# Attention: the query norm's scaling moved behind the last pass over the spikes, and one division for each group of heads

## The chip, the cores and the metric

The kernel runs on one core of a Trainium2 chip. The metric is the device time of one execution in microseconds (us). Five engines work side by side, each with its own instruction stream, and meet in semaphores: TensorE (PE; its weight loads are PEld), VectorE (DVE), ScalarE (ACT), GpSimd (POOL) and SyncE (SP), which issues the DMAs.

## The reference

One decoder layer on x (8 sequences of 512 tokens, 256 features) in three residual steps. The first is a bidirectional Mamba block with its feed-forward part. The second and third are what matters here:

```
# second: cross attention, 16 heads of 16 features, over ctx (8, 512, 256)
q = layernorm(x) @ wq.T + bq;  k = ctx @ wk.T + bk;  v = ctx @ wv.T + bv
scores = where(mask == 0, -1e9, einsum('bhqd,bhkd->bhqk', q, k) / 4)
x = x + einsum('bhqk,bhkd->bhqd', softmax(scores), v) @ wo.T + bo
# third: a spiking network, 5 steps
y = square(relu(layernorm(x) @ W_fc.T)) @ W_proj.T
mem_new = 0.9 * mem + y - (mem > 1);  spk = mem_new > 1     # five times from mem = 0
x = x + sum(spk) / 5
```

## The kernel before

A first pass does the Mamba block for all sequences and takes some 1600 us. A second, `attention_pass`, does the feed-forward part of the first step, the attention and the spiking network, one sequence (a "batch", `b` from 0 to 7) after the other. The order on every engine is written out by hand: each engine has its own function `batch(b, it, more)`, and `more` is true for the first seven, which also prepare batch b+1. Batch 0 is written out on VectorE, batches 1 to 6 run in a loop, batch 7 is written out.

In a batch TensorE first computes the scores of all 16 heads once (`prescore`), of which VectorE takes row maxima (line 1912), while the feed-forward part of the next batch is woven in. Then come eight units of four heads by half of the keys. For each, TensorE computes the scores transposed (`score`), ScalarE takes the exponential (line 1696, shown as 1633), VectorE masks one half of the keys (`keep_exp`, line 1903), and TensorE multiplies by V (`weigh`), which also gives the sum of each row from a column of ones. After each two units a group of four heads is complete: TensorE transposes it to tokens (`to_tokens`, line 1517) and VectorE divides by the sums (`normalise`, lines 1797 to 1809) into o_sb, which the trace calls x_out.

Between the masks VectorE works on other things: the spikes of the previous batch (`start`, `step`, `finish`, over tiles y_sb, mem, cnt, tmp), and the norm of the next batch's query (`norm_apply(ATT, b + 1, x1n, xn_q)`, four operations at line 1750). `finish` (line 1842) writes tmp and raises out_ready.

Behind the units TensorE projects the next batch's K in two halves (`project_k`), transposes the attention's output and then the next query (both `to_features`, line 1388), multiplies by wo, and projects V and Q. ScalarE evacuates the last group (`av`), the two halves of K into qk, the transposes into xT, in this order. The four PSUM banks for all this go round in a fixed order; the second transpose of the output uses the bank of K's first half.

The tiles mem, cnt and tmp share their memory with qk. So ScalarE's `project_k` waits until SP has stored tmp:

```
act.wait_ge(out_ready.sem, out_ready.count(beta - 1))   # ACT, line 1660
act.wait_ge(s_out.sem, s_out.count(beta - 1))           # line 1661
sp.wait_ge(out_ready.sem, out_ready.count(beta))        # SP, store(), line 1317
```

SP's order in a batch is: loads for b+2, the rows of maxima, this store, then the writes and reads that stack K and Q.

Of the kernel before, what the change touches and what calls it, by code (L numbers as in the profile page):

```python
# [14 lines left out]
H, DH = 16, 16  # L15
P = 128
KD, KI, KF, TT = D // P, DI // P, FF // P, T // P
# [64 lines left out]
def attention_keys():  # L82

    def many(kind, n):
        return [(kind, i) for i in range(n)]

    ff = many("w1", KF)
    heads = []
    for g in range(H // 4):
        heads += [("av", g)] + ([("ot", g - 1)] if g else [])  # L90
    before = many("w2", 2) + many("k", KD) + [("lo", 0)] + many("qn", KD) + many("q", KD) + [("lo", 1)] + many("v", 2)
    loop = many("hT", KD) + ff + [("w2", 0), ("mt", 0), ("w2", 1), ("mt", 1)] + heads + [("k", 0), ("ot", H // 4 - 1), ("k", 1)]
    loop += many("on", KD) + many("qn", KD) + many("wo", 2) + [("v", 0)] + many("q", KD)
    loop += many("fn", KD) + [("v", 1)] + many("fc", KF) + many("pr", 2)
    skip = ("hT", "w1", "w2", "k", "v", "qn", "q")
    return before, loop, [key for key in loop if key[0] not in skip]
# [1075 lines left out]
def attention_pass(nc, ctx, a, mid, out, sb, where, stage, psum, consts, handover, early, late):  # L1172

    f32, bf16, i32 = mybir.dt.float32, mybir.dt.bfloat16, mybir.dt.int32
    ALU, ACT, AX = mybir.AluOpType, mybir.ActivationFunctionType, mybir.AxisListType
# [15 lines left out]
    x1n = sb("x1n", [P, TT, D])  # L1191
    x1 = sb("x1", [P, TT, D])
    x_res = sb("x_res", [P, TT, D])
    xn_q = sb("xn_q", [P, TT, D])
# [15 lines left out]
    rsum = sb("rsum", [P, TT, 4])  # L1210
# [25 lines left out]
    G = Ring(general + [y_bank], kinds, B - 1, *attention_keys())  # L1236
# [15 lines left out]
    FF1, ATT, FF2 = range(3)  # L1252
# [20 lines left out]
    with nc.Block() as block:  # L1273
# [451 lines left out]
        def _(dve):  # L1725
# [6 lines left out]
            def norm_stats(n, src):  # L1732

                dve.drain()
                for j in range(TT):
                    dve.bn_stats(stats[:, j, :], src[:, j, :])  # L1736
                norm_mean(n)

            def norm_mean(n):

                dve.drain()
                for j in range(TT):
                    last = dve.bn_aggr(mv[:, j, :], stats[:, j, :])  # L1743
                last.then_inc(ln_stats[n].sem, 1)

            def norm_apply(n, beta, src, dst):

                dve.wait_ge(ln_rstd[n].sem, ln_rstd[n].count(beta))
                for j in range(TT):
                    last = dve.tensor_scalar(dst[:, j, :], src[:, j, :], mv[:, j, 0:1], rstd[:, j:j + 1],  # L1750
                                             ALU.subtract, ALU.mult)
                last.then_inc(ln_out[n].sem, 1)

            def two(ap, jj):
                return ap[:, 2 * jj:2 * jj + 2, :]

            def bank_tiles(bk):
                return bk[:, :].rearrange("p (j f) -> p j f", j=2)

            def first_norm(beta):  # L1760
                dve.wait_ge(s_x.sem, s_x.count(beta))
                settle(dve)
                norm_stats(FF1, x0)
                norm_apply(FF1, beta, x0, xn)

            def add_down(beta, it):

                dve.wait_ge(x1n_set.sem, x1n_set.count(beta))
                for jj in range(TT // 2):
                    dve.wait_ge(*G.full(("w2", jj), it))  # L1770
                    bk = G.bank(("w2", jj), it)
                    dve.tensor_tensor(two(x1n, jj), two(x1n, jj), bank_tiles(bk), ALU.add).then_inc(G.done_sem(("w2", jj)), 1)  # L1772

            def cut_lo(beta, n):
                dve.wait_ge(qk_hi.sem, qk_hi.count(4 * beta + 2 * n))
                dve.tensor_tensor(qk[:, n], qk[:, n], qk_part[:, n, 0], ALU.subtract).then_inc(qk_lo.sem, 1)

            def cut_last(beta, n):
                dve.wait_ge(qk_hi.sem, qk_hi.count(4 * beta + 2 * n + 1))
                dve.tensor_tensor(qk_part[:, n, 2], qk[:, n], qk_part[:, n, 1], ALU.subtract).then_inc(s_part.sem, 1)  # L1780
# [16 lines left out]
            def normalise(g, it):  # L1797

                dve.drain()
                dve.wait_ge(*G.full(("ot", g), it))  # L1800
                bk = G.bank(("ot", g), it)
                o = bk[:, :].rearrange("p (j h e) -> p j h e", j=TT, h=4)
                dve.reciprocal(rsum[:, :, :], o[:, :, :, DH:DH + 1].squeeze(3))
                dve.drain()
                dst = o_sb[:, :, g * 4 * DH:(g + 1) * 4 * DH].rearrange("p j (h e) -> p j h e", h=4)
                for j in range(TT):
                    last = dve.tensor_tensor(dst[:, j], o[:, j, :, 0:DH],
                                             rsum[:, j, :].unsqueeze(2).broadcast_to((P, 4, DH)), ALU.mult)
                last.then_inc(G.done_sem(("ot", g)), 1)

            def spikes(beta, cols_of=(A3,)):

# [48 lines left out]
            last = dve.tensor_scalar(keep_bf[:, :, :], maskT_i[:, :, :], 0.0, None, ALU.not_equal)  # L1861
# [29 lines left out]
            for j in range(TT):  # L1891
                last = dve.tensor_scalar(mask_bias[:, j, :], keep[:, j, :], row_keep[:, j:j + 1], None, ALU.mult)
# [5 lines left out]
            def keep_exp(b, unit):  # L1898

                kt = 2 * (unit % 2) + 1  # L1900
                dve.wait_ge(s_exp.sem, s_exp.count(b * 2 * H + unit * 4 + ON_DVE[-1]))
                exps = pr[:, ON_DVE[0]:ON_DVE[-1] + 1, kt, :]
                dve.scalar_tensor_tensor(exps, mask_biasT[:, kt, :].unsqueeze(1).broadcast_to((P, len(ON_DVE), T)), -MASKED, exps,  # L1903
                                         ALU.add, ALU.min).then_inc(s_kept_dve.sem, 1)

            def batch(b, it, more):
                for hd in range(H):
                    for j in range(TT):
                        dve.wait_ge(s_max.sem, s_max.count((b * H + hd) * TT + j - 2))
                        dve.wait_ge(s_pre.sem, s_pre.count((b * H + hd) * TT + j))  # L1910
                        settle(dve)
                        dve.tensor_tensor_reduce(  # L1912
                            masked[:, j % 2, :], bank[j], mask_bias[:, j, :], 1.0, FLOOR, ALU.add, ALU.max, m_col[:, j, hd:hd + 1]).then_inc(s_max.sem, 1)
                start, step, finish = spikes(b)
                if more:
                    add_down(b + 1, it)
                    norm_stats(ATT, x1n)
                start()
                step(1, (0,))
                keep_exp(b, 0)  # L1920
                step(1, (1, 2))
                keep_exp(b, 1)
                if more:
                    norm_apply(ATT, b + 1, x1n, xn_q)
                step(2, (0,))
                keep_exp(b, 2)
                step(2, (1, 2))
                if isinstance(it, int):
                    dve.wait_ge(early.mid.sem, early.mid.count(B))
                keep_exp(b, 3)  # L1930
                normalise(0, it)
                step(3, (0,))
                keep_exp(b, 4)
                step(3, (1, 2))
                keep_exp(b, 5)
                normalise(1, it)
                step(4, (0,))
                keep_exp(b, 6)
                step(4, (1, 2))
                keep_exp(b, 7)  # L1940
                finish()
                normalise(2, it)
                normalise(3, it)
                if more:
                    cut_lo(b + 1, 0)

                dve.wait_ge(x1_set.sem, x1_set.count(b))
                for jj in range(TT // 2):
                    dve.wait_ge(*G.full(("wo", jj), it))
                    bk = G.bank(("wo", jj), it)  # L1950
                    dve.tensor_tensor(two(x_res, jj), two(x1, jj), bank_tiles(bk), ALU.add).then_inc(G.done_sem(("wo", jj)), 1)
                    dve.drain()
                    for j in (2 * jj, 2 * jj + 1):
                        dve.bn_stats(stats[:, j, :], x_res[:, j, :])
                norm_mean(FF2)
                if more:
                    cut_last(b + 1, 0)
                    take_v(0, it)
                norm_apply(FF2, b, x_res, xn)
                if more:  # L1960
                    take_q(it)
                    cut_lo(b + 1, 1)
                    take_v(1, it)
                    cut_last(b + 1, 1)
                    dve.wait_ge(*G.done(("fn", KD - 1), it))
                    first_norm(b + 2)
# [224 lines left out]
```

## Time and profile before

| | us |
|---|---|
| median of 3 runs | 2731.34 |
| lowest and highest | 2731.16, 2732.35 |
| the profiled execution | 2730.98 |
| its span, first to last instruction | 2729.2 |
| TensorE busy | 2585.1 (95%) |
| VectorE busy | 2283.9 (84%) |
| ScalarE busy | 1743.3 (64%) |
| GpSimd busy | 1602.4 (59%) |

Times in the rows are counted from the span's start. A busy time includes work that nothing waits for, and a wait is put down to the one of several releasers that the profile shows last. A line can be that of a helper: 1380 is every matmul, 1633 every ScalarE operation of this pass, 1283 every DMA.

### The profile page before, as it was taken

The page shows a single profiled execution, that of the slowest core. Times are in us where ns is not written, and L with a number is a line of the kernel's source. Part 1 is how long each engine was busy: PE and PEld are TensorE (multiplying, and loading weights), DVE is VectorE, ACT ScalarE, POOL GpSimd, SP SyncE. Part 2 cuts the span into 40 slices and gives each one's busy share as a digit, 9 for nine tenths or more (in the row PEclk, how much of TensorE's full clock was granted, in tenths as well). Part 3 has the DMA queues.
Part 4 walks back from the last instruction along what each step waited for, and adds up shares of the span by engine and source line. Part 5 has one row for each costly group of instructions (what it writes and reads, how often), then busy time and mean ns, then how long its engine had stood idle before and what let it go on. Part 6 is the DMA issues. An engine that isn't in the chain of part 4 may idle for free. (4 is left out here: it accounts for less than half of the span.)

```text
span 2729.2 us, 54786 instructions
## 1 busy us (share of the span) xinstructions
PE 2585.1 (95%) x18901; PEld 1767.7 (65%) x18934; DVE 2283.9 (84%) x3333; ACT 1743.3 (64%) x2871; POOL 1602.4 (59%) x886
## 2 busy tenths in 40 slices
PE   6999999999999999999998888999999999999995
PEld 3887787787777778777787764455454545454523
DVE  5999999999999899999999949686869595959684
ACT  4878877877977888788788633635354545444342
POOL 3999999999999999999999932111111111111010
PEclk9999999999999999999999999999999999999978
DMA  3122212212221221222122042404040404040300
GB/s 124 43 74 79 82 48 79 92 36 72 89 72 52 81 82 44 71 82 80 50 77 98 17 152 87 114 11 123 2 123 2 123 2 123 2 123 2 108 2 16
DMA packets 102089, 187.07 MB, mean 69 GB/s; under 512 B 14720, under 2 KB 75264, under 8 KB 100256
## 3 DMA queue, kind: packets, MB, share of 16 engines
q1 hardware_dynamic: 101840, 183.92, 21.4%
q8 instruction: 135, 2.21, 0.3%
q14 instruction: 114, 0.93, 0.1%
HBM read 148.38 MB, written 35.52 MB: 67 GB/s over the span
## 5 line engine op out<-in xcount | busy, mean ns | idle before, releaser
L983 DVE TENSOR_TENSOR_SCAN h<-dA,pair 128x512 f32<-128x512 f32 x1024 | 1172.6, 1201 | 101.9 <-PE pair L476 90.6
L1122 POOL TENSOR_TENSOR hC<-h,C_rep 128x1024 f32<-128x1024 f32 x512 | 1200.8, 2370 | 72.2 <-DVE h L983 64.5
L720 ACT ACTIVATE dA<-delta,cols 128x511 f32<-128x511 f32 x1024 | 664.2, 710 | 33.8 <-DVE h L983 27.7
L476 PE MATMUL pair<-diagB,duT 64*128 64x128 f32 x8192 | 549.3, 281 | 24.9 <-DVE h L983 15.6
L476 PEld LDWEIGHTS pair<-diagB,duT 64*128 64x128 f32 x8192 | 486.4, 188 | 126.8 <-issue 96.9
L577 PE MATMUL y_bank<-ident,hC 128*128 128x128 f32 x3980 | 521.6, 277 | 12.4 <-POOL hC L1122 10.5
L577 PEld LDWEIGHTS y_bank<-ident,hC 128*128 128x128 f32 x3980 | 440.3, 141 | 105.1 <-issue 50.5
L1912 DVE CUSTOM_DVE_ANT_0 masked<-pair,mask_bias 128x512 f32<-128x512 f32 x512 | 321.8, 687 | 19.9 <-PE pair L1380 13.6
L1999 POOL TENSOR_SCALAR rstd<-mv 128x4 f32<-128x4 f32 x24 | 23.8, 992 | 453.5 <-DVE mv L1743 451.6
L1633 ACT ACTIVATE pr<-pair 128x1024 f32<-128x1024 f32 x256 | 248.4, 1022 | 50.3 <-PE pair L1380 50.2
L2028 POOL CAST m_part<-m_rest 8x512 bf16<-8x512 f32 x16 | 9.7, 604 | 415.2 <-ACT m_rest L1633 415.2
L476 PE MATMUL general<-xnT,w_in 128*128 128x512 f32 x496 | 243.0, 605 | 4.5 <-ACT xnT L720 3.6
L1380 PE MATMUL general<-w_down,g 128*128 128x256 f32 x1024 | 232.5, 380 | 1.3 <-DVEq L1728 1.3
L1380 PEld LDWEIGHTS general<-w_down,g 128*128 128x128 f32 x1024 | 193.7, 190 | 33.8 <-issue 5.9
L1380 PE MATMUL pair<-q_st,k_st 99*128 99x512 bf16 x512 | 178.5, 385 | 8.2 <-ACT pr L1633 4.7
L1380 PE MATMUL general<-xT,w_up 128*128 128x512 f32 x360 | 167.2, 601 | 1.2 <-ACT xT L1633 0.7
L1903 DVE SCALAR_TENSOR_TENSOR pr<-mask_biasT,pr 128x2048 f32<-128x2048 bf16 x64 | 153.0, 2390 | 8.5 <-ACT pr L1633 8.5
L1380 PE MATMUL pair<-k_st,q_st 96*128 96x512 bf16 x512 | 152.3, 405 | 6.0 <-DMA q_st<-qk_parts 4.2
L993 DVE SCALAR_TENSOR_TENSOR u<-general,cols,u 128x511 f32<-128x511 f32 (+2 forms) x192 | 141.7, 738 | 14.2 <-ACT u L720 10.2
L1380 PEld LDWEIGHTS pair<-q_st,k_st 99*128 99x128 bf16 x512 | 50.3, 98 | 141.4 <-ACT pr L1633 96.4
L1972 DVE COPY y_sb<-general 128x512 f32<-128x512 f32 x16 | 11.1, 691 | 139.6 <-PE general L1380 139.6
L1380 PEld LDWEIGHTS pair<-k_st,q_st 96*128 96x128 bf16 x512 | 50.1, 98 | 113.0 <-DVE m_col L1912 80.0
(185 smaller groups left out, 3240.5 us busy)
## 6 DMA issues: line engine op xcount, KB each, us to landing
C_rep<-c_rows SPq DMA_DIRECT2D x128, 512.0 KB, 4.0
qk_parts<-qk_part SPq DMA_DIRECT2D x96, 256.0 KB, 4.1
w_in<-w_in SPq DMA_DIRECT2D x16, 1024.0 KB, 4.8
k_st<-qk_parts SPq DMA_DIRECT2D x8, 1536.0 KB, 9.1
q_st<-qk_parts SPq DMA_DIRECT2D x8, 1536.0 KB, 9.4
x_in<-x SPq DMA_DIRECT2D x18, 512.0 KB, 4.1
w_out<-w_out SPq DMA_DIRECT2D x17, 512.0 KB, 4.3
mid<-x_out SPq DMA_DIRECT2D x9, 512.0 KB, 4.8
```

The lines of the kernel that those rows point to most:

```text
L476: return pe.matmul(o, lhsT, rhs, start=start, stop=stop)
L577: last = pe.matmul(y_bank[:, c * P:(c + 1) * P], hC[:, g % RING, i, c * P:(c + 1) * P], ident[:, :], start=j == 0 and i == 0 and c == 0, s ...
L720: return act.activation(o, i, fn, **kw)
L983: last = dve.tensor_tensor_scan(h[:, g % 4, i, :], dA[:, g % 4, i, :], dBu[:, i, :], 0.0, ALU.mult, ALU.add)
L993: dve.scalar_tensor_tensor(u[n][:, k, lag:T], raw[:, 0:T - lag], col("fb"[n] + "conv_w", CW * k + CW - 1 - lag), u[n][:, k, lag:T], ALU.mu ...
L1122: last = pool.tensor_tensor(hC[:, g % RING], h[:, g % 4], C_rep[:, 2 * j:2 * j + 2, :], ALU.mult)
L1380: return pe.matmul(o, lhsT, rhs, start=start, stop=stop)
L1633: return act.activation(o, i, fn, **kw)
L1903: dve.scalar_tensor_tensor(exps, mask_biasT[:, kt, :].unsqueeze(1).broadcast_to((P, len(ON_DVE), T)), -MASKED, exps, ALU.add, ALU.min).the ...
L1912: dve.tensor_tensor_reduce(masked[:, j % 2, :], bank[j], mask_bias[:, j, :], 1.0, FLOOR, ALU.add, ALU.max, m_col[:, j, hd:hd + 1]).then_in ...
L1972: dve.tensor_copy(two(y_sb, jj), bank_tiles(bk)).then_inc(G.done_sem(key), 1)
L1999: pool.tensor_scalar(rstd[:, :], mv[:, :, 1], EPS, None, ALU.add)
```

## The change

Two edits, both on VectorE. In `normalise` four multiplications, one for each block of 128 tokens, become one over 4 blocks x 4 heads x 16 features. In `batch` the query norm's four operations go from between the masks of units 1 and 2 to behind `finish`, and the division of group 2 goes from behind `finish` to ahead of it. The order at the end was mask 7, finish, normalise(2), normalise(3); it is now mask 7, normalise(2), finish, query norm, normalise(3).

```
@@ normalise
-                for j in range(TT):
-                    last = dve.tensor_tensor(dst[:, j], o[:, j, :, 0:DH],
-                                             rsum[:, j, :].unsqueeze(2).broadcast_to((P, 4, DH)), ALU.mult)
-                last.then_inc(G.done_sem(("ot", g)), 1)
+                dve.tensor_tensor(dst, o[:, :, :, 0:DH], rsum[:, :, :].unsqueeze(3).broadcast_to((P, TT, 4, DH)),
+                                  ALU.mult).then_inc(G.done_sem(("ot", g)), 1)
@@ batch
                 keep_exp(b, 1)
-                if more:
-                    norm_apply(ATT, b + 1, x1n, xn_q)
                 step(2, (0,))
@@ batch
                 keep_exp(b, 7)
+                normalise(2, it)
                 finish()
-                normalise(2, it)
+                if more:
+                    norm_apply(ATT, b + 1, x1n, xn_q)
                 normalise(3, it)
```

## Rows read from the trace of the kernel before

**Rows 1.** Page, busy time, share of the span and instructions of each engine

```profile
PE 2585.1 (95%) x18901; PEld 1767.7 (65%) x18934; DVE 2283.9 (84%) x3333; ACT 1743.3 (64%) x2871; POOL 1602.4 (59%) x886
```

**Rows 2.** Waits: us in total, times, longest us

```profile
ACT qk L1633 <- DMA out<-tmp: 20.1, 7, 2.9
```

**Rows 3.** Chain of waits, end of batch 2: start us, us, what

```profile
1997.21 1.03 ACT pr L1633
...
1998.27 2.30 DVE pr L1903
...
2000.61 1.07 PE y_bank L1380 x8
2001.68 1.91 PE general L1380 x4
...
2005.75 1.31 PE general L1388 x12
2007.06 0.44 PE y_bank L1388 x4
...
2007.51 3.73 PE general L1380 x16
```

**Rows 4.** Timeline of VectorE, batch 2: start us, us, operation, idle before

```profile
1969.47 2.28 DVE L1903 SCALAR_TENSOR_TENSOR pr<-mask_biasT,pr 128x2048 f32<-128x2048 bf16 x1
1971.67 1.38 DVE L1750 TENSOR_SCALAR xn_q<-x1n,mv,rstd 128x256 f32<-128x256 f32 x4
1973.14 1.22 DVE L1828 SCALAR_TENSOR_TENSOR tmp<-mem,y_sb 128x1024 f32<-128x1024 f32 x1
...
1979.10 2.28 DVE L1903 SCALAR_TENSOR_TENSOR pr<-mask_biasT,pr 128x2048 f32<-128x2048 bf16 x1
1981.56 0.26 DVE L1803 RECIPROCAL rsum<-general 128x16 f32<-128x16 f32 x1 [0.17 <-issue]
1981.89 0.62 DVE L1807 TENSOR_TENSOR x_out<-general,rsum 128x64 f32<-128x64 f32 x4
1982.60 1.23 DVE L1828 SCALAR_TENSOR_TENSOR tmp<-mem,y_sb 128x1024 f32<-128x1024 f32 x1
...
1998.27 2.28 DVE L1903 SCALAR_TENSOR_TENSOR pr<-mask_biasT,pr 128x2048 f32<-128x2048 bf16 x1
2000.65 1.23 DVE L1842 SCALAR_TENSOR_TENSOR tmp<-cnt,x_res 128x1024 f32<-128x1024 f32 x1
...
2004.07 0.26 DVE L1803 RECIPROCAL rsum<-general 128x16 f32<-128x16 f32 x1 [1.08 <-PE general L1517]
...
2009.58 0.68 DVE L1951 TENSOR_TENSOR x_res<-x,general 128x512 f32<-128x512 f32 x1
```

**Rows 5.** Timeline of SyncE's DMA issues, end of batch 2

```profile
2002.17 0.41 SPq L1283 DMA_DIRECT2D out<-tmp  x1
```

**Rows 6.** Timeline of ScalarE, end of batch 2

```profile
2005.22 0.69 ACT L1633 ACTIVATE qk<-general,cols 128x512 f32<-128x512 f32 x1 [2.87 <-DMA out<-tmp]
2005.80 0.68 ACT L1633 ACTIVATE qk<-y_bank,cols 128x512 f32<-128x512 f32 x1
2006.37 1.08 ACT L1633 ACTIVATE xT<-general 128x512 f32<-128x512 f32 x2
```

**Rows 7.** Line 1807 over the span: duration ns min/median/max, first and last start

```profile
L1807 DVE TENSOR_TENSOR x_out<-general,rsum x128: 211/215/226, 1714.8 to 2668.4; 128x64 f32<-128x64 f32 x128
```

**Rows 8.** Timeline of VectorE, batch 0, behind the mask of unit 3

```profile
1712.07 2.28 DVE L1903 SCALAR_TENSOR_TENSOR pr<-mask_biasT,pr 128x2048 f32<-128x2048 bf16 x1
1714.44 0.26 DVE L1803 RECIPROCAL rsum<-general 128x16 f32<-128x16 f32 x1
```

**Rows 9.** Chain of waits, end of batch 7

```profile
2667.98 0.63 DVE x_out L1807 x4
```

**Rows 10.** Windows: stretch, length, busy us of PE, PEld, DVE, ACT, POOL, PEclk, DMA

```profile
2000.00:2003.00 3.00, 2.39 (x11) 0.83 (x12) 2.66 (x7) 0.60 (x1) 0.00 (x0) 1.00 0.00 0
2665.00:2680.00 15.00, 7.18 (x39) 5.03 (x40) 7.79 (x26) 1.68 (x3) 1.26 (x2) 0.93 0.11 36
```

## The prediction

> **What bounds the kernel now.** I read the page first, then the waits, then the chain of waits through one batch, then each engine's timeline around the two places that the change touches. In the page TensorE is busy 95% of the span and VectorE 84% [rows 1]: a VectorE saving counts only where TensorE is waiting for VectorE, and an average cannot say where that is. In the waits the reader is to see one row: seven times, 2.9 us at the longest, ScalarE stood still before its write to qk until the store out<-tmp had landed [rows 2]. qk shares its memory with mem, cnt and tmp, so each of the seven batches that prepare a next one has this wait.
>
> The chain from 1997 to 2008 us is batch 2, and the batches before and after repeat it to a few hundredths. The exponentials of the last unit end at 1998.24, the mask over them (keep_exp 7) starts at 1998.27, weigh at 2000.61, then TensorE runs without a gap through K, the transposes of group 3, K again, and the transposes of line 1388, to 2007.50; the output projection starts at 2007.51 [rows 3]. Two paths end there. ScalarE's starts with the store: `finish` ends at 2000.65 + 1.23 = 2001.88 [rows 4], SP issues the store at 2002.17 [rows 5], ScalarE, idle for 2.87 us, begins K's first evacuation at 2005.22, and then works back to back (5.22, 5.80, 6.37, each 0.57 to 0.58 apart) until both xT evacuations end at 2007.45 [rows 6]. The projection needs these. So against TensorE's 2007.50 the store path has no slack worth counting: what is added to it moves the projection, and with it the residual, the second norm and the spiking network, which follow one from another.
>
> **The norm that moves (4 operations, 1.38 us).** It stands between the mask of unit 1 and step 2: the norm starts at 1971.67 and step 2 at 1973.14, where without it step 2 would start 0.09 after the mask's end at 1971.75, so it takes 1.30 us of VectorE's time there [rows 4]. Could this make the stretch shorter? Only if VectorE is still late at its end. It is not: the mask of unit 7 starts 0.03 us after the exponentials that it waits for [rows 3], VectorE has caught up by then, and an earlier start of units 2 to 5 becomes waiting for exponentials. I cost this part at nothing; if VectorE were the pacer, its whole 1.30 us would be the gain (rival 1). In the new place, behind it on VectorE stands normalise(3), counted below; its reader is query_input on TensorE, in the second half of the transposes of line 1388; its own wait for rstd is met already at the present place, some 30 us earlier.
>
> **The order of finish and normalise(2).** Before: mask ends at 2000.55, finish starts at 2000.65 (0.10 later). After: normalise(2) comes first. Its drain and wait cost what they cost behind unit 3's mask, where the mask ends at 1979.10 + 2.28 = 1981.38 and the reciprocal starts at 1981.56: 0.18. Then the reciprocal and the gap behind it, 1981.89 - 1981.56 = 0.33 [rows 4]. Then the one multiplication.
>
> **The one multiplication.** The trace has no 128x256 form of it, so it is bounded. Below by one 128x64 operation, 0.215 us [rows 7]; above by the four together, 0.62 us [rows 4]. Between them: 64 elements take 0.215 and the 128x512 tensor_tensor from PSUM of line 1951 takes 0.68 [rows 4, 7], so an element costs (0.68 - 0.215)/448 = 1.04 ns, and 256 take 0.215 + 192 x 1.04 ns = 0.42 us. I take 0.42; four small ones overlapped in 0.62, so 0.20 us is saved at each of the 32 calls. Groups 0 and 1 lie under TensorE's continuous work and give nothing.
>
> The trace has the four at 0.62 us, less than 4 x 0.215 = 0.86, so they hide part of each other's fixed time [rows 4, 7]. The Trainium skill (VectorE: DVE Perf Modes, "The TRN2 errata — SBUF-src ops pay a fixed extra latency per instruction") says that the fixed latency is exposed between instructions, so that many small tiles pay it each time, and gives (N+151)/0.96 ns for an fp32 tensor_tensor. An estimate by that page is 424 ns for the merged one and 3 x 157 ns = 0.47 us saved per call; the sum below would end 0.27 us lower, as only the last batch's tail takes it from this term, and the row for the four speaks against that larger saving.
>
> **The sum for finish.** New start of finish behind the mask's end: 0.18 + 0.33 + 0.42 + 0.09 (the gap behind normalise, from 1981.89 + 0.62 to 1982.60) [rows 4] = 1.02, against 0.10 now: 0.92 later. In batch 0, whose waits are on constants, the first gap is 1714.44 - (1712.07 + 2.28) = 0.09 instead of 0.18 [rows 8], so 0.83. The store is issued and lands that much later, and so ScalarE's K evacuation starts at 2006.14 instead of 2005.22.
>
> Does something swallow it? On TensorE the second "on" transpose takes the bank of K's first half, which ScalarE frees at 2006.14 + 0.69 = 2006.83; four transposes later (0.6 us) it is full at about 2007.45, before ScalarE comes to it at about 2007.86. So ScalarE stays back to back, ends at 2008.37, and the projection starts at about 2008.43, with TensorE idle for the difference. Nothing else ends on an absolute time there: the exponentials, masks and DMAs of K and Q all follow from this start.
>
> ScalarE's 2.87 us before K is a wait for a store and nothing else [rows 2, 6]. The Trainium skill (DMA: Bandwidth & Descriptors, "Rules for kernel authors") says to issue a DMA early and wait for its semaphore late, so that its fixed cost overlaps; this change does the reverse, putting work ahead of the issue while the waiter stays where it is. By that rule too the time comes out above the present one, and the trace agrees in that the landing ends that wait in seven of seven batches.
>
> **normalise(3).** Finish ends at 2000.55 + 1.02 + 1.23 = 2002.80. The norm starts 0.08 before that (as behind the mask, 1971.67 against 1971.75) and ends at 2004.10; with 0.17 the reciprocal is at 2004.27 against 2004.07 now, and the multiplication ends at 2004.27 + 0.33 + 0.42 = 2005.02, where the four end now (2004.07 + 0.33 + 0.62) [rows 4]. No change; and the transposes of line 1388 now have most of a microsecond to spare before ScalarE wants them.
>
> **The last batch** has no norm and no K to evacuate, so the late store costs nothing there. Its chain runs through normalise(3), whose multiplications take 0.63 us there before the transposes [rows 9]. In either order the same operations stand ahead of it, less 0.20 us for group 2, so VectorE comes to it no later than now, and the shorter multiplication counts: -0.2.
>
> **Sum.** 0.83 + 6 x 0.92 - 0.2 = 6.15 us, on a profiled execution of 2730.98 (span 2729.2, the rest around it unchanged). The profiled run lies 0.36 below the median of 2731.34; carried to the median, 2737.5 us. The unknown multiplication gives the narrow range: at 0.215 it is 1.4 less in seven batches and 0.2 less in the last, 2735.9; at 0.62 it is 1.4 more, and the last saving is gone, 2739.1.
>
> **Rivals.** Rival 1, faster: VectorE is the pacer of the spikes stretch. Taking 1.30 us out before unit 2 then brings the last mask 1.30 forward, more than the 0.92 that the store loses; net 0.38 per batch, 7 x 0.38 + 0.2 = 2.9, so 2728.5. It decides from the point where the last mask starts more than 0.92 earlier relative to the exponentials. For it: it is busy 84% of the span, and more in this stretch than in most. Against it: the 0.03 us at the last mask, where ScalarE is the releaser [rows 3].
>
> Rival 2, no change: the store was hidden anyway, the wait put down to it having really ended with something else, such as TensorE's K in y_bank. Then only the -0.2 is left, 2731.1. For it: TensorE ends K's second half at 2005.75, close to its evacuation at 2005.80 [rows 3, 6]. Against it: the first half was complete at 2001.68 + 1.91 = 2003.59, and its evacuation waited 1.6 us more, until the store landed.
>
> Rival 3, slower still: the merged operation, with its three strides and its broadcast, costs what the four cost or more, or the longer gap takes something from TensorE's clock. The price of the first is 2739.1. For the clock: it stayed at 1.00, that is 2.4 GHz, in the three microseconds with the 1.1 us gap before weigh, and showed 0.93 only where TensorE was busy for 7.18 of 15 us [rows 10]; an added gap of 0.9 us is nearer to the first.
>
> **Chances.** Forecast 0.76, rival 1 0.06, rival 2 0.10, rival 3 0.08. The time is the forecast's, 2737.5. The range for 8 in 10 is 2734.0 to 2739.5: it holds the forecast with its bounds and most of rival 3, goes a little towards rival 2 for a partial cover of the store, and leaves out the rest. 0.2%, about what a measurement of this kernel can tell from no change, is 5.5 us, and the lower part of the forecast's range lies within that. So faster 0.06, same 0.10 + 0.14 of the forecast's 0.76 = 0.24, slower 0.70.
>
> **What would show it.** Right: finish ends some 2.25 us behind the last mask's end instead of 1.33; out<-tmp is issued 0.9 us later relative to that mask, and ScalarE's idle time before qk grows from 2.9 to about 3.8 us; the projection of w_att and xT starts about 10.2 us behind the last mask's start instead of 9.24, with a new TensorE idle time before it that ScalarE's xT ends; line 1807 has 32 rows of 128x256 at about 0.42; a batch takes 0.9 us more. The masks of units 2 to 5 start earlier, the last one does not. Wrong: if the last mask stands earlier against its exponentials, rival 1; if the store moves and the projection does not, rival 2; if line 1807 shows 0.6 or more, or the clock falls between 2003 and 2009 us, rival 3. A span that is less than 4 us longer would mean that a cover exists which I have not seen.

## The result, and the profile after

The kernel after takes 2741.2 us at the median of 11 runs (2735.37 to 2745.24), the one before 2731.52 (2728.81 to 2733.72, 11 runs): a ratio of 1.0033 with a 95% interval of 1.0025 to 1.0041, about 9 us more. The profiled execution took 2741.24 us, its span is 2739.5 us, 10.3 more than before. The forecast was 2737.5 in 2734.0 to 2739.5: the right way, and too small.

The chain of waits of the kernel after through the end of batch 2 (start, us, what) answers to [rows 3]:

```profile
1997.42 1.03 ACT pr L1633
...
1998.48 2.29 DVE pr L1901
...
2000.93 0.26 DVE rsum L1803
...
2001.26 0.42 DVE x_out L1806
...
2001.78 1.24 DVE tmp L1840
...
2003.31 2.94 DMA out<-tmp
...
2006.35 0.70 ACT qk L1633
...
2007.09 1.09 PE general L1388 x8
2008.19 0.44 PE y_bank L1388 x4
...
2008.65 3.50 PE general L1380 x15
```

Before, this chain went through TensorE's own queue. It now leaves the mask through the division of group 2 and through `finish` into the store, and comes back to TensorE through ScalarE's K evacuation. From the mask's start to the projection it takes 2008.65 - 1998.48 = 10.17 us, against 9.24. The timelines of VectorE, ScalarE and TensorE in the same place answer to [rows 4, 6]:

```profile
1998.48 2.29 DVE L1901 SCALAR_TENSOR_TENSOR pr<-mask_biasT,pr 128x2048 f32<-128x2048 bf16 x1
2000.93 0.26 DVE L1803 RECIPROCAL rsum<-general 128x16 f32<-128x16 f32 x1 [0.16 <-issue]
2001.26 0.42 DVE L1806 TENSOR_TENSOR x_out<-general,rsum 128x256 f32<-128x256 f32 x1
2001.78 1.23 DVE L1840 SCALAR_TENSOR_TENSOR tmp<-cnt,x_res 128x1024 f32<-128x1024 f32 x1
2002.92 1.38 DVE L1750 TENSOR_SCALAR xn_q<-x1n,mv,rstd 128x256 f32<-128x256 f32 x4
2004.47 0.26 DVE L1803 RECIPROCAL rsum<-general 128x16 f32<-128x16 f32 x1 [0.16 <-PE general L1517]
```

```profile
2006.35 0.69 ACT L1633 ACTIVATE qk<-general,cols 128x512 f32<-128x512 f32 x1 [3.80 <-DMA out<-tmp]
2006.94 0.68 ACT L1633 ACTIVATE qk<-y_bank,cols 128x512 f32<-128x512 f32 x1
2007.51 1.09 ACT L1633 ACTIVATE xT<-general 128x512 f32<-128x512 f32 x2
```

```profile
2007.09 0.66 PE L1388 MATMUL general<-ident,x_out 128*128 128x128 f32 x4 [0.70 <-ACT qk L1633]
```

The merged multiplication takes 0.42 us, `finish` ends 2.24 us behind the last mask, and ScalarE waits 3.80 us instead of 2.87. TensorE stands still 0.70 us ahead of the second "on" transpose, until ScalarE frees its bank. That is its only added wait: ahead of the projection the weight loads wait 0.26 us for xT, and in the kernel before 0.25. Two paths meet at the projection again, TensorE's transposes (to 2008.63) and ScalarE's xT (to 2008.60).

But a batch is longer by more than these 0.93 us. The store's issue marks one point in every batch: 1868.66 and 2003.31 here, so 134.65 us apart; before, 1868.66 and 2002.17, 133.51 apart. The six periods differ by 1.12 us each. The other 0.19 is in the stage of the maxima. The timeline of VectorE after, batches 1 to 3, shows the same pause there in each:

```profile
1811.01 0.69 DVE L1910 CUSTOM_DVE_ANT_0 masked<-pair,mask_bias 128x512 f32<-128x512 f32 x1 [0.41 <-issue]
...
1945.65 0.69 DVE L1910 CUSTOM_DVE_ANT_0 masked<-pair,mask_bias 128x512 f32<-128x512 f32 x1 [0.42 <-issue]
...
2080.29 0.69 DVE L1910 CUSTOM_DVE_ANT_0 masked<-pair,mask_bias 128x512 f32<-128x512 f32 x1 [0.42 <-issue]
```

"Issue" says that the engine waited for nothing that the profile shows. The kernel before has no such pause in its loop. Two more of this kind stand in the kernel after. The first is in batch 0 alone, ahead of `finish`, and makes the store there later: it is issued 5.09 us behind the mask's start instead of 3.90, and the projection starts at 10.43 instead of 9.25, so batch 0 loses 1.18 us. The second is in every batch of the loop, ahead of the reciprocal behind the mask of unit 3, where the kernel before has 0.17:

```profile
1732.51 1.23 DVE L1840 SCALAR_TENSOR_TENSOR tmp<-cnt,x_res 128x1024 f32<-128x1024 f32 x1 [0.45 <-issue]
...
1981.08 0.26 DVE L1803 RECIPROCAL rsum<-general 128x16 f32<-128x16 f32 x1 [0.52 <-issue]
```

And the last batch is longer too: from its last mask's start to the end 2739.5 - 2668.2 = 71.3 us, before 2729.2 - 2662.8 = 66.4. Windows over its last mask, then the output projection, then the first W_fc matmuls (columns as in [rows 10]), first after, then before:

```profile
2668.20:2677.00 8.80, 5.41 (x31) 2.66 (x29) 4.87 (x7) 1.79 (x3) 0.00 (x0) 0.74 0.18 60
2677.00:2683.50 6.50, 6.44 (x16) 4.86 (x16) 1.46 (x4) 0.00 (x0) 0.00 (x0) 0.57 0.00 0
...
2691.20:2699.10 7.90, 7.90 (x13) 3.47 (x14) 0.00 (x0) 2.45 (x4) 0.00 (x0) 0.68 0.00 0
```

```profile
2662.80:2670.50 7.70, 4.08 (x32) 1.62 (x30) 5.29 (x13) 1.68 (x3) 0.00 (x0) 1.00 0.20 68
2670.50:2674.20 3.70, 3.70 (x16) 2.94 (x16) 1.44 (x3) 0.00 (x0) 0.00 (x0) 1.00 0.00 0
...
2682.00:2688.80 6.80, 6.79 (x13) 3.08 (x14) 0.00 (x0) 2.45 (x4) 0.00 (x0) 0.79 0.00 0
```

The same sixteen matmuls take 6.5 us at a clock of 0.57 (near 1.2 GHz) and 3.7 at 1.00 (2.4 GHz).

So the 10.3 us between the two profiles have three parts: -2.3 up to the last mask of batch 0, 7.7 from there to the last mask of batch 7, 4.9 from there to the end. The first part lies ahead of every instruction that the change touches: in the profiles of all thirteen kernels here this mask starts between 1728.2 and 1733.9 us, and always 58.1 us behind the same row of maxima, so the difference arises before that row, and the first division comes later. What makes it is open.

### The profile page after: what moved, and what is told of

It reads as the page before. It is cut to its first block and busy times, and to the rows that moved or that the text cites. A ratio compares the mean times of both kernels' runs of the same rounds, so it can differ in the third digit from the quotient of the medians.

```text
span 2739.5 us, 54723 instructions
## 1 busy us (share of the span) xinstructions
PE 2589.7 (95%) x18934; PEld 1769.4 (65%) x18934; DVE 2278.6 (83%) x3237; ACT 1743.3 (64%) x2871; POOL 1602.1 (58%) x886
```

## The experiments

Four theories. S: the loss is the store, issued behind more work while ScalarE waits for it ahead of K. R: it is the norm's or the division's own cost. I: the 0.19 us per batch is a pause of VectorE's instruction supply, which depends on where its code lies. C: what is left is TensorE's clock in the last batch. Ratios are against the kernel before on the same chip.

**The swap alone.**

```
                 keep_exp(b, 7)
+                normalise(2, it)
                 finish()
-                normalise(2, it)
                 normalise(3, it)
```

> The kernel before with one edit: normalise(2) stands ahead of finish; four multiplications, and the query norm, stay as they were. Theory S (the late store): finish comes 0.18 + 0.33 + 0.62 + 0.09 - 0.10 = 1.12 us later behind the last mask, so out<-tmp is issued 5.0 us behind that mask's start instead of 3.9, ScalarE waits 4.0 us for it instead of 2.9, the projection starts 10.4 us behind the mask instead of 9.24, and each of seven batches is 1.1 us longer: 7.8 us in all. Theory R (the moved norm or the merged division makes the loss): no change. Theory C (TensorE's clock in the last batch makes what lies above 6.5 us): 7.8 us as in S, and more only if the profile shows half the clock behind the last batch's masks.

Measured: 2742.21 us (5 runs), ratio 1.0038 [1.0024, 1.0051]. The store is issued 5.02 us behind the mask's start, ScalarE waits 4.00 us for it, the projection starts 10.36 behind, the periods are 134.63, 1.12 more: every length as S has it. There is no pause among the maxima in the loop, and in the last batch of its profile the clock is near half over the output projection (0.57), which may be what lies above 2731.1 + 7.8 = 2738.9. The swap alone makes a loss as large as the whole change; with four multiplications ahead of `finish` the store alone costs 1.12 us a batch, with the one it is 0.93.

**The norm alone.**

```
                 keep_exp(b, 1)
-                if more:
-                    norm_apply(ATT, b + 1, x1n, xn_q)
...
                 finish()
                 normalise(2, it)
+                if more:
+                    norm_apply(ATT, b + 1, x1n, xn_q)
                 normalise(3, it)
```

> The kernel before with one edit: the query norm goes behind normalise(2), ahead of normalise(3), and finish stays directly behind the last mask. Theory S: the store is issued as before (3.9 us behind the mask's start), so only normalise(3) can be late: the norm ends near 6.0 us behind the mask's start, normalise(3) near 7.15 instead of 6.75, the transposes wait some 0.3 us, and a batch is 0.3 us longer, 2 us in all. Theory R: the whole loss of the change, 1.1 us per batch, stands here. Rival 1 of the prediction (VectorE is the pacer): faster by up to 1.3 us per batch.

Measured: 2731.33 (11 runs), 1.0002 [0.9993, 1.0011], periods of 133.51. R is out for the norm, and so is the prediction's first rival: 1.30 us taken from the spikes' stretch brought nothing. My own 0.3 us was wrong: normalise(3) does end 7.12 us behind the mask's start instead of 6.75, as worked out, but the transposes start 7.31 behind, as before. There was more slack there than I had read from the weight loads.

**The division alone**, as in the first part of the diff.

> The kernel before with one edit: one multiplication of 128x256 in each normalise. Theory S: the store and the projection stay where they are; the last batch saves 0.2 us; no change in all. Theory I (VectorE has 12 operations fewer in a batch, its code lies elsewhere, and the stall of 0.42 us among the maxima in each batch of the loop comes from that): that stall, shown as masked <- issue, appears here too, and a batch is up to 0.2 us longer, 1.3 us in all. Against I: no such stall, period 133.5 us.

Measured: 2732.3 (11 runs), 1.0003 [0.9994, 1.0012]. In the total nothing is seen, but the periods are 133.71 instead of 133.51, with the pause of 0.42 us in every batch of the loop: the first sign for I. It comes with the merge, not with the moves, and so does the one ahead of `finish` in batch 0 (0.44 us; the projection starts 9.59 us behind the mask instead of 9.25). The second pause of the loop, ahead of the reciprocal, is not here; e4 below has it with the same period, so it costs nothing that shows. The division as work of the engine costs nothing either, and R is out for it too.

**The store waited for where it must be.** The kernel after with

```
 def project_k(beta, it):
-    act.wait_ge(s_out.sem, s_out.count(beta - 1))
...
 for k in range(KD):
     evacuate(("on", k), xT[1][:, k, :], it)
 if more:
+    act.wait_ge(s_out.sem, s_out.count(b))
     high(b + 1, 0)
```

> The kernel after, but ScalarE's wait for the store moves from ahead of its K evacuations to ahead of the first copy into qk_part, which is what shares memory with tmp; K's half of qk shares it with mem alone, and mem is read for the last time before out_ready. Theory S: ScalarE evacuates K's first half when finish is done (near 2.3 + 2.25 - 0.0 = 4.6 us behind the mask's start, instead of 7.9), the projection starts 9.25 us behind the mask as in the kernel before, and the loss of 0.93 us per batch is gone: 6.5 us less than the kernel after, so 0 to +3 against the one before. What is left is the 0.19 us per batch of the maxima's stall (1.3 us) and, by theory C, the clock in the last batch (up to 4 us in one run). Rival (the loss sits in the transposes' late input, not in the store): as slow as the kernel after.

The timeline of ScalarE in batch 2 of this kernel; its last mask starts 5.36 us before the first line:

```profile
2004.03 0.69 ACT L1633 ACTIVATE qk<-general,cols 128x512 f32<-128x512 f32 x1 [1.29 <-PE general L1380]
2006.18 0.69 ACT L1633 ACTIVATE qk<-y_bank,cols 128x512 f32<-128x512 f32 x1 [1.47 <-PE y_bank L1380]
2006.77 1.07 ACT L1633 ACTIVATE xT<-general 128x512 f32<-128x512 f32 x2
```

K is now evacuated when TensorE has made it. The store is still issued 4.82 us behind the mask's start, as late as in the kernel after, and the projection starts 9.23 behind, as in the kernel before; periods are 133.70. The 0.93 us are gone though every VectorE operation stands where the change put it, which settles S. The total is 2736.58 (11 runs), 1.0017 [1.0008, 1.0026], some 4.6 us above the kernel before, where 6 x 0.19 = 1.1 are the pause. The rest is not in the periods; the profile has 1.7 us of it behind the store that is issued in batch 7 (below, "the last store"; two half-size ones follow at the very end).

**The instruction stream as long as before.** The kernel after with

```
 dve.tensor_tensor(dst, o[:, :, :, 0:DH], ...)
+for _ in range(TT - 1):
+    settle(dve)          # a semaphore increment
```

> The kernel after, with three semaphore increments (sequencer instructions, no work of the engine) behind each merged multiplication, so that VectorE's instruction stream is as long as before at the same places. Theory I (the stall of 0.42 us among the maxima in each batch of the loop comes from where VectorE's code lies, the stream being shorter by three instructions at each normalise): the stall is gone, a batch takes 134.45 us instead of 134.64, and 1.3 us are gone in all. Rival (it comes from the moved norm, or from the timing of the batch): the stall stays, at the same place; e3 with the merged division alone speaks against that. A third outcome: the increments cost some 0.05 us each on the way to finish, and the store is later by up to 0.15 us, a batch longer by as much.

Measured: 2736.89 (9 runs), 1.0022 [1.0012, 1.0032]. All three pauses are gone, in batch 0 and in the six batches of the loop; the periods are 134.42, 0.21 less, and batch 0's projection starts 10.09 us behind the mask, 0.84 later than in the kernel before. In its profile TensorE's clock is 1.00 over the last output projection (16 matmuls in 3.72 us), and from the last store to the end it takes 62.57 us, as in the kernel before. The store is issued 4.83 us behind the mask's start, so the increments cost nothing that shows. The same in the kernel with the division alone:

> e3 (the merged division alone) with three semaphore increments behind each merged multiplication, as in e5. Theory I: no stall among the maxima in the loop, a batch takes 133.51 us as in the kernel before instead of 133.71, and with the store in its place nothing else is left: 2731.0 plus or minus 1. If the merged division itself cost something: 133.7 us.

Measured: 2730.98 (11 runs), 0.9994 [0.9985, 1.0003], periods of 133.52. So the part of I that was tested holds: twelve instructions more or fewer per batch turn the pause off and on. That it is a wait for code is argued only. Which instruction meets it, and whether it is the code's address or the distance between two loads of code, I did not separate. The Trainium skill (Runtime: NRT & Kernel Launch, "Instruction fetch mechanics") says that each engine's sequencer fetches its code in blocks with DMAs of its own, and that crossing a block is mostly hidden. Here, if that is what the pause is, 0.42 us of it showed in each batch, 0.19 to 0.21 of which reached the period.

**The last batch as before.** The kernel after, but with the old order and the four multiplications in batch 7:

```
+if more:
+    normalise(2, it); finish(); norm_apply(ATT, b + 1, x1n, xn_q)
+else:
+    finish(); normalise(2, it)
```

> The kernel after, but in the last batch alone the order (finish, then normalise(2)) and the four multiplications are as before. Theory P (the last batch is slower in the kernel after, 4 us in its profile, because the clock's falls land at another moment, which the earlier batches' length decides): as slow as the kernel after, 2741, low mean clock in as many runs, and half the clock in the profile behind the last masks. Rival L (the last batch's own order or its merged operation does it): the time falls by about 2 us at the median and the clock behind the last masks is 1.00 as in the kernel before.

Measured: 2742.09 (5 runs), 1.0042 [1.0028, 1.0056], with the clock over the output projection near half again. The last batch's own edits are not what makes it slow.

**TensorE kept busy in the last batch.**

```
 def prescore(b, hd):
+    if isinstance(b, int) and b == B - 1:
+        mm(bank[j], ...)                    # each prescore twice
...
+if not more:
+    pe.wait_ge(*G.free(("fn", 0), it))
+    for _ in range(16):
+        mm(G.bank(("fn", 0), it)[:, :], ident_bf[:, :], mask_biasT[:, 0, :])
 pe.wait_ge(ln_out[FF2].sem, ln_out[FF2].count(b))
```

> The kernel after, with TensorE kept busy in the last batch alone: each prescore matmul is issued twice, and 16 matmuls of 128x512 bf16 go into the bank of the norm's transposes before it is waited for; outputs are unchanged. Theory C (what lies above 7 x 1.12 us in the kernel after is TensorE at 1.2 instead of 2.4 GHz behind the last masks): the clock shows 1.00 from the prescores of the last batch to the end of its matmuls but for the last spikes, the spread of the runs shrinks to 5 us or less, and the median falls by 3 to 6 us, to 2735 to 2738. If the clock were no cause, the median stays at 2741 or rises by what the added matmuls take (up to 1 us).

Windows of this kernel over the output projection and the first W_fc matmuls:

```profile
2673.40:2677.10 3.70, 3.68 (x16) 3.11 (x18) 1.44 (x3) 0.00 (x0) 0.00 (x0) 1.00 0.01 4
...
2684.00:2689.40 5.40, 5.39 (x13) 2.52 (x14) 0.00 (x0) 2.45 (x4) 0.00 (x0) 1.00 0.00 0
```

Measured: 2734.59 (11 runs), 1.0017 [1.0008, 1.0026], 4.4 us below the kernel after by the ratios and 6.6 by the medians (two chips), with more matmuls than it has. From the last store to the end it takes 59.35 us, where the kernel after takes 66.75 and the one before 62.67. The maxima gain too: the last store comes 129.40 us behind the one before it, against 130.92. The spread did not shrink as expected (2731.55 to 2739.98), so the clock in the last batch is not all that makes it. The same added to the kernel before:

> The kernel before with TensorE kept busy in the last batch as in e7. Theory C: the last batch is worth the same to both kernels once the clock is at 2.4 GHz, so what is left between this and e7 (2734.6) is the seven batches' 7 x 1.12 = 7.8 us less 0.2 to 0.4 for the last batch's shorter division: 2727.0. From its parts: issue to issue as in the kernel before (133.5), the last store to the end 59.5 us instead of 62.7. If the clock's fall were tied to the kernel after alone, this would stay at 2731.

Measured: 2729.59 (11 runs), 0.9988 [0.9979, 0.9997], 2.6 above what I expected; the last store to the end is 60.41 us in the profile, not 59.5. So the clock costs the kernel before something as well. With it kept up, after and before are 1.0017 - 0.9988 = 0.0029 apart, 7.9 us, where the lengths in the traces give 6 x 1.12 + 1.18 - 0.2 = 7.7; without, 0.0033, 9.0 us. The clock's share of the difference is thus about 1 us by the ratios, and 3 by the medians (9.7 - 6.4); with intervals of some 2.5 us on each ratio, that it is more than nothing isn't shown.

**A version below both.** Two paths end at the projection, so both must be shortened. The kernel before, with ScalarE's wait as in e4, and half of K's first projection in the gap in which TensorE waits for the last mask:

```
 if unit + 1 < H // 2:
     score(b, unit + 1, half)
+elif more and half == 1:
+    project_k_part(b + 1, 0, 0, it)      # K's first half, k = 0
 weigh(b, unit, half, it)
...
 if more:
-    project_k(b + 1, 0, it)
+    project_k_part(b + 1, 0, 1, it)      # k = 1
```

> The kernel before (its order on VectorE untouched), with ScalarE's wait for the store ahead of its first copy into qk_part, as in e4, and on TensorE the first half of K's first projection (k = 0, 0.86 us) ahead of the last weigh, where TensorE stands still 1.13 us for the last mask. Theory S (two paths end at the projection, the store's and TensorE's own): both are shortened by this, the projection starts 8.4 to 8.5 us behind the last mask's start instead of 9.24, a batch takes 132.7 us, and the kernel 5.5 us less than before, 2725 to 2726, less what the clock in the last batch adds (up to 4 us in a run). If the store were no bound: the same. If ScalarE's evacuation of the last group now ends last: 9.0 to 9.2 us, and 1 us gained at most.

TensorE's timeline there; the last weigh no longer shows a wait:

```profile
1995.90 1.13 PE L1380 MATMUL general<-ctxT,w_att 128*128 128x512 f32 x2
1997.10 1.07 PE L1380 MATMUL y_bank<-pr,v_sb 128*32 128x512 f32 x8
1998.10 1.12 PE L1380 MATMUL general<-ctxT,w_att 128*128 128x512 f32 x2
```

Measured: 2728.13 (11 runs), 0.999 [0.9981, 0.9999]; the projection starts 8.37 us behind the mask's start and the periods are 132.64, 0.87 less. Of the 6.1 us in seven batches only 2.8 reach the median: from the last store to the end the profile shows 67.68 us instead of 62.67. With TensorE kept busy in the last batch as well:

> e8 (half of K's projection in TensorE's gap, the store waited for later) with TensorE kept busy in the last batch as in e7. Both parts are in different batches and add up: 6 periods of 132.64 instead of 133.52 us, and the last store to the end 59.5 us instead of 62.7: 2721 to 2722, some 9.5 us below the kernel before. If the clock eats the gain of e8 in another way: 2725 or more.

Measured: 2722.68 (6 runs), 0.9967 [0.9955, 0.9979], 9 us below the kernel before, which makes this version the fastest of all. From the last store to the end its profile has 62.09 us, not the 59.5 expected: the clock was not 1.00 throughout.

## Why the prediction was wrong in size and right in kind

1. That ScalarE's wait for the store sets the pace at the end of a batch, with no slack against TensorE's own path: right. Shown by e1 (the swap alone makes the loss) and e4 (moving the wait alone takes it away). Rival 2 is out.
2. The lateness of `finish`, 0.92: right, measured 0.93 in the loop. In batch 0, 0.83 was forecast; without the pauses it is 0.84 (e5), with them 1.18. ScalarE's K was due 7.87 us behind the mask's start and started 7.87 behind in batch 2; the multiplication was taken at 0.42 and took 0.42. The added wait of TensorE is not ahead of the projection, where the prediction put it, but ahead of the second "on" transposes, at K's bank; the time of the projection comes out the same (10.17 us behind the mask's start, 10.16 forecast).
3. The moved norm at nothing: right (e2). The last masks start 0.03 us behind their exponentials in both kernels; what VectorE gained became waiting, such as 0.76 us ahead of the mask of unit 6. Rival 1 is out.
4. normalise(3) at no change: right for its effect, and with more room than I claimed (e2).
5. The step that failed is the sum, in "the rest around it unchanged": it put everything outside the edited stretch at nothing, without a reason. Two things changed there. The merged division made VectorE's instruction stream shorter, and pauses appeared: 0.42 us among the maxima of each batch in the loop, of which 0.19 reached the period, and 0.45 ahead of `finish` in batch 0, of which 0.35 reached the projection; 6 x 0.19 + 0.35 = 1.5 us in all. I had counted the edit's instructions as engine time only, not as code. Shown by e3, e5 and e11. Without the pauses the kernel after is at 1.0022, which is 6.0 us, where the forecast had 6.15. That this comes so close is in part luck: the interval is 2.7 us to either side, and the profile of e5 has the clock at 1.00 over the last output projection, as the kernel before has.
6. The second thing is the clock. The last batch was put at -0.2; in the profile it took 4.9 us more from its last mask to the end, where the output projection ran at 0.57. The clock stood in rival 3, as something that an added gap in the middle might take. In the middle it stayed at 1.00. The prediction read that the kernel before showed less than 1.00 only where TensorE was busy for 7.18 of 15 us; that overlooks the last batch's maxima, where both kernels have 0.50 from 2600 to 2610 us with TensorE busy throughout. What the clock adds to the difference of the medians is not fixed: 1 to 3 us, and nothing is within the intervals. That the last batch's own edits are not the cause is shown (e6 has the fall without them, e5 has them without the fall); it is not the pauses either, as e1 has the fall and no pause. That the length of the earlier batches decides, by moving the moment, fits e3, e6 and e8, whose profiles have near half the clock too with no common edit in that batch, and is argued only, from one profile of each.
7. The range ended at 2739.5, 1.7 us below the median. It was built from the terms of the sum alone. The spread of single runs, 5 us before and 10 us after, was not in it, and up to the last mask of batch 0 alone single profiles differ by 5.7 us.

## What to carry to other kernels

A write that another engine waits for, through a buffer that two tiles share, belongs ahead of work that nobody waits for; and the wait belongs ahead of the first instruction that touches the shared bytes, not ahead of the stage. Before counting a VectorE saving, look at what ends the wait behind it: here 1.3 us per batch were free, and 0.9 of store latency were not. Fewer instructions can also cost: after an edit that changes their number, look for new idle time put down to "issue" at the same place of every pass. In a kernel whose tail runs with gaps in TensorE's work, leave a few us in the range for the clock there, and measure a period inside the loop beside the total.

## What the runs showed of the hardware

Twelve VectorE instructions fewer in a loop body of some 133 us turned on a pause of 0.42 us per pass; three semaphore increments in the place of each three multiplications turned it off, at no cost that shows (e5, e11). A pause of 0.52 us elsewhere in the same pass cost nothing: periods 133.70 with it (e4) and 133.71 without (e3).

Four operations of 128x64 in a row take 0.62 us and one of 128x256 takes 0.42, though each small one is shown at 0.215.

The runs of the kernel after had mean clocks from 0.980 to 0.985, and the longest had the lowest: 2745.24 at 0.980, 2735.37 at 0.985. Added matmuls whose results are thrown away made the kernel before faster by 0.12% [0.03, 0.21] (e9).
